# Turning the normed tiles of a flamingo block's loop by DVE squares and a gather through device memory

## The reference

```
x = x + tanh(g_xattn) * (softmax(q k^T / sqrt(128) + bias, masked) v) Wo     # q from layernorm(x), k and v from the context, 32 heads of 128
x = x + tanh(g_ffn)   * (layernorm(x) W^T + bias + lora(layernorm(x)))       # lora: rank 16, three adapters, chosen per batch
```

## Time and profile before

| | |
|---|---|
| median of 3 runs | 1750.52 us |
| profiled execution | 1750.89 us, span 1749.0 us, mean granted TensorE clock 0.997 |
| PE busy | 1723.6 us, 99% of the span |
| DVE busy | 1231.2 us, 70% |
| ACT, POOL busy | 619.5 us and 613.1 us, 35% each |
| DMA | 336.5 MB, SP's queue 54.3% of 16 engines |
| chain that ended last | PE 93%, DVE 3%, POOL, ACT, DMA and issue 1% each |

### The profile page before, as it was taken

One profiled execution on the slowest core, in us unless ns is written; L12 is line 12 of the kernel. 1 busy time (PEld: TensorE's weight loads), 2 busy tenths in 40 slices (PEclk: granted clock), 3 DMA queues, 4 the chain that ended last, 5 costly groups with the idle time before them and its releaser, 6 DMA issues.

```text
span 1749.0 us, 25056 instructions
## 1 busy us (share of the span) xinstructions
PE 1723.6 (99%) x8656; PEld 1463.3 (84%) x8656; DVE 1231.2 (70%) x2649; ACT 619.5 (35%) x1225; POOL 613.1 (35%) x811
## 2 busy tenths in 40 slices
PE   6999999999999999999999999999999999999998
PEld 5888888788888888888888888888888888888887
DVE  6777777877777775677767776567776777666674
ACT  4544445444333332233333333223333333333321
POOL 4565656654233222233223232223332322222221
PEclk9999999999999999999999999999999999999999
DMA  7777677766545544545545454355455454454531
GB/s 276 261 263 271 245 268 271 275 231 229 192 159 190 188 157 162 193 163 193 180 162 193 169 185 176 139 193 187 175 178 183 169 193 162 158 192 162 176 128 46
DMA packets 111456, 336.50 MB, mean 192 GB/s; under 512 B 13361, under 2 KB 13489, under 8 KB 111330
## 3 DMA queue, kind: packets, MB, share of 16 engines
q1 hardware_dynamic: 111186, 334.63, 54.3%
q10 hardware_dynamic: 144, 0.26, 0.0%
HBM read 263.54 MB, written 71.30 MB: 191 GB/s over the span
## 4 chain that ended last, share of the span: by engine, by line
PE 93%; DVE 3%; issue 1%; POOL 1%; DMA 1%; ACT 1%; SPq 0%; ACTq 0%; DVEq 0%; POOLq 0%
PE vo_bank L297 13%; PE vo_bank L295 13%; PE vo_bank L296 13%; PE q_bank L295 7%; PE q_bank L297 7%; PE q_bank L296 7%; PE k_bank L297 6%; PE k_bank L295 6%; PE k_bank L296 6%; PE pv_two L300 5%; PE s_two L300 5%; PE pv_two L301 2%; PE s_two L301 2%; PE vo_bank L573 1%; DVE score L918 0%
## 5 line engine op out<-in xcount | busy, mean ns | idle before, releaser
L1153 POOL TENSOR_TENSOR score<-score,row_max 128x256 f32<-128x256 f32 x128 | 78.6, 614 | 820.2 <-DVE row_max L923 820.1
L1096 POOL TENSOR_TENSOR ot_lo<-attn,ot_hi 128x512 fp32r<-128x512 f32 x128 | 165.6, 1294 | 151.6 <-ACT ot_hi L669 151.6
L295 PE MATMUL q_bank<-xt_hi,wq 128*128 128x512 f32 x512 | 208.7, 408 | 0.0
L295 PE MATMUL k_bank<-ct_hi,wk 128*128 128x512 f32 x512 | 200.4, 391 | 6.2 <-DVE ct_lo L850 6.2
L297 PE MATMUL q_bank<-xt_hi,wq 128*128 128x512 f32 x512 | 200.8, 392 | 0.0
L296 PE MATMUL k_bank<-ct_lo,wk 128*128 128x512 f32 x512 | 200.2, 391 | 0.0
L296 PE MATMUL q_bank<-xt_lo,wq 128*128 128x512 f32 x512 | 200.2, 391 | 0.0
L297 PE MATMUL k_bank<-ct_hi,wk 128*128 128x512 f32 x512 | 200.2, 391 | 0.0
L295 PE MATMUL vo_bank<-wv,ct_hi 128*128 128x512 f32 x504 | 196.3, 389 | 0.0
L296 PE MATMUL vo_bank<-wv,ct_hi 128*128 128x512 f32 x504 | 196.2, 389 | 0.0
L297 PE MATMUL vo_bank<-wv,ct_lo 128*128 128x512 f32 x504 | 196.2, 389 | 0.0
(11 more groups left out here) (198 smaller groups left out, 3740.7 us busy)
## 6 DMA issues: line engine op xcount, KB each, us to landing
wv<-wv_split SPq DMA_DIRECT2D x96, 512.0 KB, 5.3
wq<-wq_split SPq DMA_DIRECT2D x96, 512.0 KB, 3.2
wk<-wk_split SPq DMA_DIRECT2D x96, 512.0 KB, 3.6
wo<-wo_split SPq DMA_DIRECT2D x96, 512.0 KB, 5.0
raw_bias<-in_pair_bias SPq DMA_DIRECT2D x64, 256.0 KB, 5.9
wq_split<-wq SPq DMA_DIRECT2D x32, 512.0 KB, 2.9
wk_split<-wk SPq DMA_DIRECT2D x32, 512.0 KB, 4.1
wv_split<-wv SPq DMA_DIRECT2D x32, 512.0 KB, 6.0
```

Of the source, the lines that this page charges most:

```text
L295: pe.matmul(to, left[0], right[0], start=first, stop=False)
L1096: pool.tensor_tensor(to, src, f32(of), ALU.subtract).then_inc(done, 1)
L1153: pool.tensor_tensor(score[:, :, :], score[:, :, :], row_max[:, :].unsqueeze(2).to_broadcast([P, PB, S]), ALU.subtract).then_inc(shift_don ...
```

## The change

The 24 turns of the loop leave PE. DVE still normalises, into `xn[0]`, and then turns the 32 x 32 squares of the tile in place into `xn[1]` by one transpose instruction. At the end of its turn for this slot SP saves `xn[1]` to `squares[u]` in device memory (256 KB; `save_squares`, u counts the turns). At the very beginning of its next slot SP waits for that save and until POOL is done with the tile before (`moved_lo` at u), and issues four DMAs that gather the squares into the single tile `xg`, in its turned place (`gather_squares`). Each writes 32 partitions from pieces of 32 floats (128 bytes): 512 pieces each, 2048 for a tile. ACT rounds the high part from `xg` at the end of its slot n + 1 (`moved`), POOL takes the low part after `add_bias` of its slot n + 2 (`moved`). DVE no longer takes that low part. The turns move to slots 7, 8, 9, 10 and 24, 25, 27, 28 of a block. Before the loop and after it the turns stay on PE.

```diff
--- before.py
+++ after.py
@@ -40,8 +40,8 @@
 LEAD, FFN = 0, 1
 
 
-FFN_SUMS, FFN_PIECES, FFN_TURNS, LORA, DENSE = (5, 6), (7, 8, 11, 12), (9, 10, 13, 14), (15, 16), (17, 18, 19, 20)
-X_LOAD, LEAD_SUMS, LEAD_PIECES, LEAD_TURNS = 21, (22, 25), (23, 24, 27, 28), (25, 26, 29, 30)
+FFN_SUMS, FFN_PIECES, FFN_TURNS, LORA, DENSE = (5, 6), (7, 8, 11, 12), (7, 8, 9, 10), (15, 16), (17, 18, 19, 20)
+X_LOAD, LEAD_SUMS, LEAD_PIECES, LEAD_TURNS = 21, (22, 25), (23, 24, 27, 28), (24, 25, 27, 28)
 LORA_PIECES = (5, 6)
 
 
@@ -53,6 +53,9 @@
     if n < SLOTS and b < BLOCKS - 1 and s in LEAD_TURNS:
         return LEAD, b + 1, LEAD_TURNS.index(s)
     return None
+
+
+TURNS = [turn_at(n) for n in range(SLOTS) if turn_at(n)]
 
 
 def sums_at(n):
@@ -121,8 +124,6 @@
         found += [("v", values_at(n)[0], t) for t in values_at(n)[1]]
     if output_at(n):
         found += [("o", output_at(n)[0], t) for t in output_at(n)[1]]
-    if turn_at(n):
-        found += [("turn", *turn_at(n))]
     if lora_at(n):
         found += [("lora", *lora_at(n))]
     if dense_at(n):
@@ -190,6 +191,8 @@
         wv_split, wo_split = (nc.dram_tensor(f"w{m}_split", [FIRST_GROUPS * G, P, 2 * D], F32, kind="Internal").ap()
                               for m in "vo")
 
+        squares = nc.dram_tensor("squares", [len(TURNS), P, D], F32, kind="Internal").ap()
+
         qt = two("qt", [P, BLK])
         kt = sb("kt", [P, PB, 2, P], F32R)
         v = two("v", [P, 3, PB, G * DH // 2])
@@ -213,6 +216,7 @@
 
         stage = [sb(f"stage{i}", [P, 512]) for i in range(2)]
         xn = [sb(f"xn{i}", [P, D]) for i in range(2)]
+        xg = sb("xg", [P, C, P])
         lo_t = two("lora", [P, 2, PAIR])
         stats = sb("stats", [P, PB, 6])
         mean_var = sb("mean_var", [P, PB, 2])
@@ -252,6 +256,8 @@
             sem(f"{m}_lo") for m in ("q", "k", "pt", "ot", "wq", "wk", "wv", "wo", "stage", "lead_ct", "lora"))
         wq_saved, wk_saved, wv_saved, wo_saved, wq_back, wk_back, wv_back, wo_back = (
             sem(f"w{m}_{w}") for w in ("saved", "back") for m in "qkvo")
+        squared, squares_saved, moved_in, moved_hi, moved_lo = (
+            sem(m) for m in ("squared", "squares_saved", "moved_in", "moved_hi", "moved_lo"))
         vo_free, ot_b, ot_sum, acc_done = sem("vo_free"), sem("ot_b"), sem("ot_sum"), sem("acc_done")
         gate_done, exp_done, var_done, pow_done, bias_done = (
             sem(f"{m}_done") for m in ("gate", "exp", "var", "pow", "bias"))
@@ -399,6 +405,18 @@
                     load(to[:, :], wf[s], done)
                 else:
                     load(to[:, :], ctxt[C * (b + 1) + s - 4], done)
+
+            def save_squares(u):
+                sp.wait_ge(squared, u + 1)
+                load(squares[u], xn[1][:, :], squares_saved)
+
+            def gather_squares(u):
+
+                sp.wait_ge(squares_saved, 16 * (u + 1))
+                wait(sp, moved_lo, u)
+                for j in range(C):
+                    sp.dma_start(xg[cols(j, P // 4), :, :].rearrange("c k (i s) -> c k i s", i=4),
+                                 squares[u].rearrange("(i c) (k j s) -> j c k i s", i=4, k=C, j=4)[j]).then_inc(moved_in, 16)
 
             def store(b, t):
                 sp.wait_ge(vo_free, NUMBER["dense", b, t] + 1)
@@ -427,6 +445,8 @@
                 load(wv_split[c], f32(flat(v_both[:, c, :, :])), wv_saved)
             for n in range(SLOTS):
                 b, s = divmod(n, H)
+                if turn_at(n - 1):
+                    gather_squares(TURNS.index(turn_at(n - 1)))
                 if n > 0:
                     save_pair(n - 1)
                 if n + 2 <= H:
@@ -444,6 +464,8 @@
                     piece(3)
                 elif at:
                     piece(at[0] + 2)
+                if turn_at(n):
+                    save_squares(TURNS.index(turn_at(n)))
                 if dense_at(n):
                     store(*dense_at(n))
                 if s == X_LOAD and b < BLOCKS - 1:
@@ -464,8 +486,10 @@
         def _(pe):
             def queries(n):
                 b = n // H
-                if n % H == 0:
+                if n == 0:
                     pe.wait_ge(vo_free, NUMBER["turn", LEAD, b, PB - 1] + 1)
+                elif n % H == 0:
+                    pe.wait_ge(moved_lo, TURNS.index((LEAD, b, PB - 1)) + 1)
                 if n < H:
                     pe.wait_ge(wq_lo, n + 1)
                 else:
@@ -575,7 +599,11 @@
 
             def lora_inner(b, p):
                 job = ("lora", b, p)
-                wait(pe, vo_free, max(FREED[job], NUMBER["turn", FFN, b, 2 * p + 1] + 1))
+                if b < END:
+                    wait(pe, vo_free, FREED[job])
+                    pe.wait_ge(moved_lo, TURNS.index((FFN, b, 2 * p + 1)) + 1)
+                else:
+                    wait(pe, vo_free, max(FREED[job], NUMBER["turn", FFN, b, 2 * p + 1] + 1))
                 if b == 0:
                     pe.wait_ge(stage_lo, 4)
                 for c in range(C):
@@ -608,8 +636,6 @@
                 keys(n)
                 main_job(n, 0)
                 main_job(n, 1)
-                if turn_at(n):
-                    turn(*turn_at(n))
                 if lora_at(n):
                     lora_inner(*lora_at(n))
                 if dense_at(n):
@@ -748,6 +774,13 @@
                 act.wait_ge(vo_ps, NUMBER[job] + 1)
                 hi(xt[b % 2][0][:, :, cols(t, P)], by(bank_of(job), C), vo_hi)
 
+            def moved(norm, b, t):
+                u = TURNS.index((norm, b, t))
+                if norm == LEAD and b > 1 and t == 0:
+                    act.wait_ge(vo_ps, NUMBER["dense", b - 2, PB - 1] + 1)
+                act.wait_ge(moved_in, 64 * (u + 1))
+                hi(xt[b % 2][0][:, :, cols(t, P)], xg[:, :, :], moved_hi)
+
             def piece(n):
                 z, what, c = piece_at(n)
                 b = n // H
@@ -792,6 +823,8 @@
                 exps(n)
                 if n > 0:
                     attention(n - 1)
+                if turn_at(n - 1):
+                    moved(*turn_at(n - 1))
 
             def load(to, src, done):
                 act.dma_start(to, src).then_inc(done, 16)
@@ -950,10 +983,22 @@
                 if t >= 2:
                     dve.wait_ge(vo_ps, NUMBER["turn", norm, b, t - 2] + 1)
                 elif r > 0:
-                    before = [job for job in ALL_JOBS if job[0] == "turn" and run(job[1], job[2]) == r - 1]
-                    dve.wait_ge(vo_ps, NUMBER[before[t + 2]] + 1)
+                    dve.wait_ge(squared, len(TURNS))
+                    dve.wait_ge(squares_saved, 16 * len(TURNS))
                 dve.tensor_scalar(xn[t % 2][:, :], acc[b % 2][:, t, :], mean_var[:, t, 0:1], rstd[:, t:t + 1],
                                   ALU.subtract, ALU.mult).then_inc(xn_done, 1)
+
+            def normalise_squares(norm, b, t):
+                u, r = TURNS.index((norm, b, t)), run(norm, b)
+                dve.wait_ge(rstd_done, 2 * r + t // 2 + 1)
+                if u == 0:
+                    dve.wait_ge(vo_ps, NUMBER["turn", LEAD, 0, PB - 1] + 1)
+                wait(dve, squared, u)
+                dve.tensor_scalar(xn[0][:, :], acc[b % 2][:, t, :], mean_var[:, t, 0:1], rstd[:, t:t + 1],
+                                  ALU.subtract, ALU.mult).then_inc(xn_done, 1)
+                dve.wait_ge(xn_done, PB * r + t + 1)
+                wait(dve, squares_saved, 16 * u)
+                dve.transpose(xn[1][:, :], xn[0][:, :]).then_inc(squared, 1)
 
             def turn(norm, b, t):
                 job, at = ("turn", norm, b, t), (slice(None), slice(None), cols(t, P))
@@ -1013,12 +1058,10 @@
                 if sums_at(n):
                     statistics(*sums_at(n))
                 if turn_at(n):
-                    normalise(*turn_at(n))
+                    normalise_squares(*turn_at(n))
                 if n > 0:
                     main_job(n, 0)
                     main_job(n, 1)
-                if turn_at(n):
-                    turn(*turn_at(n))
                 if lora_at(n):
                     lora_gate(*lora_at(n))
                 if dense_at(n):
@@ -1148,6 +1191,11 @@
                     to = ct[(b - 1) % 2] if what == "dense" else ct[(b + 1) % 2]
                     lo(to[1][:, c, :], stage[z % 2][:, :], to[0][:, c, :], stage_lo)
 
+            def moved(norm, b, t):
+                u = TURNS.index((norm, b, t))
+                pool.wait_ge(moved_hi, u + 1)
+                lo(xt[b % 2][1][:, :, cols(t, P)], xg[:, :, :], xt[b % 2][0][:, :, cols(t, P)], moved_lo)
+
             def shift(n):
                 pool.wait_ge(max_done, n + 1)
                 pool.tensor_tensor(score[:, :, :], score[:, :, :],
@@ -1171,6 +1219,8 @@
                 if n % H == 0:
                     masks(n // H)
                 add_bias(n)
+                if n > 1 and turn_at(n - 2):
+                    moved(*turn_at(n - 2))
                 if n + 1 < H:
                     weights_q(n + 1)
```

## The result

The changed kernel takes 1786.74 us as the median of 4 runs (1781.25 to 1789.49), the kernel before beside it 1751.63 us (1750.33 to 1754.66, 4 runs): a ratio of 1.019, 95% interval 1.018 to 1.021, so 2% slower. The forecast was 1759 with a range up to 1788: the direction was right, the size a quarter of what came.

A forecast was written before the change was run, and what follows sets the result against it. PE, busy 99% of the span, was taken as the bound. Losses of 16.6 + 3.4 + 5.1 + 1.5 = 26.6 us against 18.2 gained gave +8.4, so 1759 us, 0.5% slower, range 1738 to 1788.

The forecast's parts named there:

- PE's gain: In the 24 turned slots, PE gets back 7.9 + 3.7 + 6.6 = 18.2 us if no new wait comes.
- the mechanism and its places: SP's queue: gathers waiting for POOL delay the `wq` load, issued at 10.95, so PE stalls before queries at ten places.
- 0.65 + 3 x 0.8: On SP's queue: issuing the four gathers of a tile takes 3.1 us, ahead of the `wq` load.
- 0.55 for normalising: On DVE in a turned slot: normalising takes 0.55 us, so DVE reaches the scores at 12.2, nothing late.
- the stalls: PE before the queries: 10 x 1.4 + 2 x 1.3 = 16.6 us lost to late `wq` loads.
- It lands 3.2 us later: The `wq` load lands 3.2 us after issue; issued at 10.95 it lands at 14.15, 1.4 us late.
- the clock: PE's lower clock after stalls: 3.4 us for two of 2.7, 5.1 for three of the eight of 1.4.
- block 0: Block 0: raw weights pushed some 4 us later, counted as 1.5 us lost, range 0 to 3.
- the gathers push what follows, the raw weights: SP's queue in block 0: raw weights for the slot after next move to about 13, some 4 us later.
- Fast issue: Rival on SP's queue: gathers issue as fast as ordinary DMAs, 0.42 each, giving 1736 to 1753 us; chance 0.36.
- Slow pieces: Rival in the DMA engines: short pieces make `wq` land 4.2 us late, giving 1771 to 1798 us; chance 0.19.
- DVE or ACT as a bound: Rival: turned slots stay at 13.2 and the stalls come on top, some 1768 us; chance 0.05.

The follow-up runs named there:

- e10: e9 without saves and gathers, ACT and POOL reading the squares where they stand, so the tile is not turned; 1733.69 us, ratio 0.989.
- e3: The changed kernel with one plain load of 256 KB for the four gathers, all waits kept, output lacking the turning; 1746.59 us, ratio 0.997.
- e1: The changed kernel with a second gather tile `xg`, so SP waits only for the tile before the last; 1743.66 us, ratio 0.995.
- e6: e4 without saves and gathers, ACT and POOL reading the squares where they stand, so the tile is not turned; 1738.83 us, ratio 0.993.
- e4: The changed kernel, one tile, with turns in every second slot (7, 9, 11, 13 and 23, 25, 27, 29); 1740.15 us, ratio 0.993.
- e12: e9 with gathers on ACT's queue, two behind the high parts of `wo`, two behind the probabilities; 1734.61 us, ratio 0.991.
- e9: e4 with block 0's lead turns in slots 18, 21, 26, 29, none beside `wo`, its x load and statistics earlier; 1738.71 us, ratio 0.992.

## Why the prediction was right and wrong

**Right: PE's gain.** 18.2 us by the sum; e10 has 17.1 of them, and turned slots last 12.76. The other 1.1 stand in slot 25 of block 0, where PE waits 0.77 us for POOL's `ot_lo` though e10 has no turn there: not quite all of the 6.6 was due to the instruction that is gone.

**Right: the mechanism and its places.** SP waits for POOL's low part, gathers stand ahead of `wq`, and PE stalls at the ten places named, not at the second gated slot of a run. The issue of `wq` stands at 11.01 in slot 41, forecast 10.95. That is partly luck: four gathers take 2.61, not 3.1 ("0.65 + 3 x 0.8"), since each takes the 0.65 of the lora row and the slow follower is `wq`, 0.62 for 0.33; and POOL frees the tile at 8.29, not 7.85. The save of the squares lands 4.0 us after its issue (median of 24), not 2.0; where the gather waits for POOL, that costs nothing.

**Why POOL is 0.45 late.** The step "0.55 for normalising" failed. In 12 of the 24 turns it takes 1.38 or 1.39:

```profile
535.24 1.39 DVE L997 TENSOR_SCALAR xn<-acc,mean_var,rstd 128x512 f32<-128x512 f32 x1
536.66 0.71 DVE L1001 STREAM_TRANSPOSE xn<-xn 128x512 f32<-128x512 f32 x1
```

and POOL beside it:

```profile
535.05 1.29 POOL L1139 TENSOR_TENSOR ct_lo<-stage,ct_hi 128x512 fp32r<-128x512 f32 x1 [2.76 <-ACT ct_hi L695]
```

In all 12 a subtraction of POOL on SBUF began 0.19 us earlier; where there is none, as in slot 41, it takes 0.55. In slot 25 of block 0 POOL was 0.72 us into one, and it took 0.85: in all 13 it ended 0.28 or 0.29 us after POOL's. The new slots 7, 8, 24, 27 and 28 are those in which POOL splits the context of the next block. So DVE reaches the scores at 12.95 of slot 40 (551.76), not at 12.2. "SBUF — State Buffer" of the Trainium skill, under "Who interferes with whom", has VectorE and GpSimd share one pair of ports, for some instructions of VectorE, and whoever issues first gets it for the whole instruction. The trace agrees: 0.55 became 1.39.

**Wrong in size: the landing, and with it the stalls (16.6 by the sum, 26.2 measured, +9.6).** "It lands 3.2 us later" took the median of a quiet queue. Behind four gathers that have just been issued it was 4.32 in slot 41, and from issue to next query 3.8 to 5.4 in the ten. Of all 96 `wq` loads the 20 right behind gathers land after 4.4 us (median), the other 76 after 3.2; in e3, behind one plain load, the 20 land after 3.7. So about 0.5 of the 1.2 us come with any load just ahead, and 0.7 with the pieces. PE's idle times ahead of the queries are 2.2, 1.5, 3.9, 2.0 in block 1, 3.0, 1.5, 4.3, 2.5 in block 2 and 2.5, 1.1 in block 3, together 24.6: on the whole 0.8 longer than forecast each. Each also costs 0.16, since the first query starts 0.06 us behind the start of the matmul before it where nothing is late, but only behind its whole 0.22 after a stall: 1.6 in all.

**Right in size: the clock (8.5; 9.1 measured, +0.6).** The five slots that ran in part at the lower clock behind these stalls are 1.6, 2.3, 1.5, 2.1 and 1.6 us longer. The two long stalls cost 2.3 and 2.1, where I gave them 1.7; of the eight others three dropped the clock (2.2, 2.0 and 2.5 us of idle time) and 3.0 and 2.5 in block 2 did not. Three was the number that I had taken, but no row stood behind it: that is luck. Stalls near this length sometimes drop it and sometimes not, which fits the 8 us between the runs of this kernel; the runs that were not traced leave that open. The last 1.2 of the 36.5 us are not the stalls': slot 9 is 0.2 to 0.4 longer, others a little, and e1, without these stalls, has 1.2 as well.

**Wrong: block 0 (1.5, range 0 to 3; measured 10.0, +8.5).** The mechanism stood there ("the gathers push what follows, the raw weights"), the room was guessed, and it is nil. In slot 26 SP is released at 9.6, and behind the gathers the two issues of a save take 1.10 and the next 1.97 (0.32 in the earlier trace rows), so the raw weights are asked for at 367.17, 15.4 us into the slot; before they followed the save of `wq` at 8.6. That is over 6 us later, not 4. ACT and DVE in slot 27, which starts at 364.55:

```profile
371.57 0.63 ACT L695 ACTIVATE wq<-raw_q 128x512 fp32r<-128x512 f32 x1 [2.45 <-DMA raw_q<-in_wq]
...
375.73 0.69 DVE L883 TENSOR_TENSOR wo<-raw_vo,wo 128x512 fp32r<-128x512 f32 x1 [5.89 <-ACT wo L695]
```

That slot alone has 5.2 us of excess. PE idles for 3.43 us there, and the 6.8 us at the lower clock behind it cost as much again, half of that in slot 28; slots 25 and 29 have 1.6 each. And the gain of 6.6 was counted in full, though turns beside DVE's `wo` cost about 4 by themselves in the slots of e6; the change's own slots were not run without DMAs.

The account: 9.6 (stalls) + 0.6 (clock) + 1.2 (slot 9 and others) + 8.5 (block 0) + 1.9 (the start) = 21.8, which is 30.2 less 8.4. The medians differ by 35.1, 5 more, since the profiled run is the fastest of its kernel.

**The rivals.** Fast issue was wrong: 0.65 for each gather. Slow pieces was wrong in size, though its 1771 to 1798 holds the result: a gather of 512 pieces lands in 2.5 us (median of 96), a tile costs the DMA engines 0.7 us more than a plain load (e3), and `wq` behind it lands 0.7 later, not 3. The pieces do go slowly: in the trace of the change a packet of 128 bytes takes one of the 16 engines 12.8 ns (49152 packets), one of 2048 bytes 93.6 ns (35377), so 10 bytes per ns against 22. The rule of "DMA: Bandwidth & Descriptors" of the Trainium skill (Specifications) on transfers below 512 bytes has them below the line rate, and there the trace agrees; that they are read, modified and written no run here shows. At 256 KB a tile it is little, and what they load most is the issuing queue. DVE or ACT as a bound: not in blocks 1 to 3 (e4 has 0.3), but DVE is one in block 0. The rule of "VectorE: DVE Perf Modes" of the Trainium skill (rules for kernel authors) that a 128x128 transpose goes to TensorE speaks against what e12 shows to pay: 0.71 us on an engine that is 70% busy is cheaper than 0.44 on the one that is 99%.

## What to carry to other kernels

Work taken off the bounding engine is not free until its messages are: count every issue and every wait that is put on a shared in-order queue, and ask what stands behind it. A queue that waits for a single buffer holds up every load behind it; a second buffer, or the same work spaced further apart, each removed over 35 us of excess here, and an idle engine's queue another 5.7 (4.1 between the medians of e9 and e12). Before giving a late load "some room", look for an engine that has it in the middle of a fixed order: here the room was nil.

## What was not expected of the hardware

- An issue of 512 pieces of 128 bytes takes 0.64 us of the queue (0.57 to 0.69 in 96), about as long as one of 512 pieces of 192 bytes and twice as long as a plain one of 256 KB (0.33); the plain issue right behind four of them takes 0.62 for 0.33.
- A DMA packet of 128 bytes took 12.8 ns of its engine, one of 2048 bytes 93.6 ns.
- One instruction of DVE on SBUF operands took 0.55 or 1.39, and the low part of `wo` mostly 0.69, but 1.65, the longer one whenever POOL was 0.19 us into a subtraction of 1.29. The squares' transpose took 0.71 or 0.72 in all 24.
- Idle times of PE of 2.0 us dropped the granted clock to 0.50 for 3.4 us once, and of 3.0 us did not.
